# Cross-attention queries for pairs of tiles from float32r parts, rows normalised two tiles ahead, later weights loaded between the first contexts

## The chip, the core and the metric

The kernel runs on one core of a Trainium2 chip. The metric is the device time of one execution in microseconds (us). A core has TensorE (PE, with its weight loads shown as PEld), VectorE (DVE), ScalarE (ACT), GpSimd (POOL) and SyncE (SP), each with its own queue of instructions. They meet through semaphores only. SP and ACT issue the transfers from memory here.

## The reference

64 batches with 64 rows of x and 256 context rows each, 256 channels, 16 heads of 16. Three residual steps follow one another, all in float32:

```python
x = x + xattn(_layernorm(x), ctx, ctx, Wq, bq, Wk, bk, Wv, bv, Wo, bo)
x = x + attn(_layernorm(x), w_qkv, b_qkv, w_out, b_out)      # causal, 64 x 64
x = x + ffn(_layernorm(x), w_gate, w_up, w_down)             # quantised gate/up/down
# xattn
q = (queries @ Wq.T + bq).reshape(B, L, H, E)
k = (keys @ Wk.T + bk).reshape(B, S, H, E)
v = (values @ Wv.T + bv).reshape(B, S, H, E)
scores = jnp.einsum('blhe,bshe->bhls', q, k)
attn = jax.nn.softmax(scores * scale, axis=-1)
out = jnp.einsum('bhls,bshe->blhe', attn, v).reshape(B, L, H * E)
return out @ Wo.T + bo
```

## The kernel before

A tile is two batches, 128 rows; there are NT = 32 tiles. The kernel runs three stages after each other, each over all tiles: cross-attention, self-attention, feed-forward. x_all holds all rows between them. The order of the instructions on each engine is written out by hand, in one `body` per engine; no scheduler moves them. Every step waits for named semaphores.

In cross-attention a tile t has two halves s, one batch each. The steps of TensorE, by function, in the order of its `body(t)`:

- `pe_k` and `pe_v` (L287, L302) project a context half to keys and values. The context c_sb is split by `act_c` (L463, ScalarE) into a rounded float32r part ch, and by `pool_c` (L505, GpSimd) into the rest cl = c_sb - ch. Three products (high by high, high by low, low by high) then stand for the full one: 12 matmuls of 256 columns.
- `pe_xt` (L267) turns the normalised rows xn of tile t + 1. `act_xt` (L455) copies them to xnT, and `pe_q` (L274) makes q for the same tile with 8 fp32 matmuls of 128 columns. `dve_q` (L408) adds the bias, applies the head mask and writes qb in four operations.
- `pe_scores` (L318) writes four banks of scores, `dve_max` (L448) takes the maxima, `act_exp` (L488) makes eight exponentials with their sums, `pe_transpose` (L331) turns four pairs of them, `dve_pt` and `act_pt` (L417, L469) copy those to probsT.
- `pe_pv` (L354) multiplies by V; `pe_r` (L341) turns the inverse sums that `pool_rm` (L512) spreads; `dve_o` forms oT; `pe_out` (L364) projects it to y_ps and `dve_y` (L441) adds it to x_all.
- `dve_stats`, `pool_rstd` and `dve_xn` normalise x of tile t + 1 from the one buffer x_sb; `pool_xb` (L500) adds the output bias.

xt_ps and y_ps share one half of PSUM bank 3, q_ps is the other half. Beside this, tiles 1 to 6 sum the absolute feed-forward weights on ScalarE (`act_wabs`), tiles 9 to 20 round one piece of them each on VectorE (L558, L564, L569), and tiles 22 to 24 split the self-attention weights. SP issues x and the contexts for the next tile (L1076, L1082). Before its loop it issues the loads of the later stages, SET2 and SET3 (L1069, L1071), 4.3 MB.

## Time and profile before

| what | value |
|---|---|
| median of 3 runs | 943.34 us (943.32 to 947.49) |
| profiled execution, its own time | 944.46 us |
| its span, first to last instruction | 942.3 us |
| mean granted TensorE clock | 0.993 of 2.4 GHz |
| PE busy | 883.0 us, 94% |
| DVE busy | 774.7 us, 82% |
| ACT busy | 679.1 us, 72% |
| POOL busy | 408.9 us, 43% |
| transfers | 31.67 MB, mean 34 GB/s |

The share of busy time says which engine has the most work, not which one is waited for. The cross-attention stage fills the first 558 us of the span. The chain of work that the page follows back from the end covers 9% of the span, all in the last stage, so it says nothing of the stage that is changed; there the waits and the order in time have to be read.

### The profile page before, as it was taken

The page shows a single profiled execution, that of the slowest core. Times are in us where ns is not written, and L with a number is a line of the kernel's source. Part 1 is how long each engine was busy: PE and PEld are TensorE (multiplying, and loading weights), DVE is VectorE, ACT ScalarE, POOL GpSimd, SP SyncE. Part 2 cuts the span into 40 slices and gives each one's busy share as a digit, 9 for nine tenths or more (in the row PEclk, how much of TensorE's full clock was granted, in tenths as well). Part 3 has the DMA queues.
Part 4 walks back from the last instruction along what each step waited for, and adds up shares of the span by engine and source line. Part 5 has one row for each costly group of instructions (what it writes and reads, how often), then busy time and mean ns, then how long its engine had stood idle before and what let it go on. Part 6 is the DMA issues. An engine that isn't in the chain of part 4 may idle for free. (4 is left out here: it accounts for less than half of the span.)

```text
span 942.3 us, 28985 instructions
## 1 busy us (share of the span) xinstructions
PE 883.0 (94%) x9714; PEld 722.8 (77%) x9730; DVE 774.7 (82%) x1650; ACT 679.1 (72%) x2013; POOL 408.9 (43%) x611
## 2 busy tenths in 40 slices
PE   5899999999999999999999988999999995999996
PEld 4688888888888888888888876878878773555554
DVE  3787878888988888888888887988888886999995
ACT  3587787676776777767767675777777765888886
POOL 1222322223223222233332226766767642767775
PEclk9999999999999999999999999999999998999999
DMA  8111111111111111111111100000000000000010
GB/s 303 38 40 39 33 39 40 46 39 34 39 39 34 38 39 45 39 33 39 39 43 35 33 1 1 1 3 0 1 0 1 2 1 1 24 31 32 29 34 33
DMA packets 31623, 31.67 MB, mean 34 GB/s; under 512 B 3281, under 2 KB 30801, under 8 KB 31569
## 3 DMA queue, kind: packets, MB, share of 16 engines
q1 hardware_dynamic: 30720, 30.73, 10.6%
q8 instruction: 20, 0.33, 0.1%
q10 hardware_dynamic: 848, 0.33, 0.1%
q14 instruction: 35, 0.28, 0.1%
HBM read 26.86 MB, written 4.19 MB: 33 GB/s over the span
## 5 line engine op out<-in xcount | busy, mean ns | idle before, releaser
L488 ACT ACTIVATE probs<-psum,nmax 128x256 f32<-128x256 f32 x512 | 237.3, 488 | 90.1 <-DVE nmax L448 90.1
L448 DVE TENSOR_REDUCE nmax<-psum 128x2 f32<-128x512 f32 x256 | 159.0, 683 | 30.7 <-PE psum L318 30.7
L331 PE MATMUL psum<-id_sb,probs 128*128 128x128 f32 x1024 | 136.1, 276 | 14.1 <-ACT probs L488 14.0
L331 PEld LDWEIGHTS psum<-id_sb,probs 128*128 128x128 f32 x1024 | 111.6, 141 | 29.8 <-ACT probs L488 28.7
L496 POOL TENSOR_TENSOR rstd<-vare,minus_half 128x1 f32<-128x1 f32 x96 | 52.6, 548 | 183.9 <-DVE vare L385 181.3
L505 POOL TENSOR_TENSOR cl<-c_sb,ch 128x512 fp32r<-128x512 f32 x64 | 81.4, 1272 | 98.4 <-ACT ch L463 98.4
L488 ACT ACTIVATION_READ_ACCUMULATOR probs<-psum,nmax 128x1 f32 x512 | 112.7, 220 | 0.0
L469 ACT ACTIVATE probsT<-psum 128x512 f32<-128x512 f32 x160 | 90.7, 620 | 9.1 <-PE psum L331 9.1
L512 POOL TENSOR_TENSOR rm<-rinv,hm_sb 128x256 f32<-128x256 f32 x64 | 39.7, 620 | 129.0 <-DVE rinv L424 129.0
L318 PE MATMUL psum<-k_sb,qb 32*128 32x256 f32 x1024 | 78.4, 404 | 0.0
L354 PE MATMUL psum<-probsT,v_sb 128*32 128x128 f32 x2048 | 69.5, 277 | 0.0
L354 PEld LDWEIGHTS psum<-probsT,v_sb 128*32 128x32 f32 x2048 | 52.3, 110 | 21.4 <-issue 15.4
L395 DVE TENSOR_TENSOR v_sb<-psum,bv_sb 128x512 f32<-128x512 f32 x64 | 44.2, 691 | 24.1 <-PE psum L302 24.0
L417 DVE COPY probsT<-psum 128x512 f32<-128x512 f32 x96 | 62.7, 653 | 0.0
L1031 PE MATMUL psum<-wb_all,xqT 128*128 128x512 bf16 x240 | 58.9, 388 | 3.9 <-PEq L1058 2.6
L836 POOL TENSOR_TENSOR kbd<-c_sb,qm_sb 128x1024 f32<-128x1024 f32 x32 | 60.6, 1893 | 3.0 <-ACT c_sb L786 3.0
L318 PEld LDWEIGHTS psum<-k_sb,qb 32*128 32x128 f32 x1024 | 51.1, 186 | 11.2 <-issue 5.9
L302 PE MATMUL psum<-wvh,ch 128*128 128x256 f32 x256 | 59.5, 313 | 0.0
L455 ACT ACTIVATE xnT<-psum 128x256 f32<-128x256 f32 x32 | 12.2, 382 | 62.5 <-PE psum L267 62.5
L287 PE MATMUL psum<-ch,wkh 128*128 128x256 f32 x256 | 56.8, 303 | 0.0
L816 ACT ACTIVATE sc<-sc 128x1024 f32<-128x1024 f32 x32 | 33.8, 1058 | 28.0 <-DVE sc L741 28.0
L287 PE MATMUL psum<-cl,wkh 128*128 128x256 f32 x256 | 51.7, 284 | 0.0
(131 smaller groups left out, 2316.3 us busy)
## 6 DMA issues: line engine op xcount, KB each, us to landing
c_sb<-in_ctx_t SPq DMA_DIRECT2D x64, 256.0 KB, 2.7
x_sb<-in_x SPq DMA_DIRECT2D x32, 128.0 KB, 2.0
out<-y_sb SPq DMA_DIRECT2D x32, 128.0 KB, 1.7
w_all<-in_w_gate SPq DMA_DIRECT2D x1, 1024.0 KB, 8.6
w_all<-in_w_up SPq DMA_DIRECT2D x1, 1024.0 KB, 10.9
w_all<-in_w_down SPq DMA_DIRECT2D x1, 1024.0 KB, 13.1
wqkv_sb<-in_w_qkv SPq DMA_DIRECT2D x1, 768.0 KB, 6.5
wq_sb<-in_wq ACTq DMA_DIRECT2D x1, 256.0 KB, 3.8
```

Of the source, the lines that this page charges most:

```text
L287: last = nc.tensor.matmul(k_ps[:, m, :], w[:, k, cols], c[s][:, k, :], start=n + k == 0, stop=n == 2 and k == KT - 1)
L302: last = nc.tensor.matmul(v_ps[:, kh, :], c[s][:, k, keys], w[:, k, :], start=n + k == 0, stop=n == 2 and k == KT - 1)
L318: last = nc.tensor.matmul(sp[c][:, m * S:(m + 1) * S], qb[m][rows, s, :, :].rearrange("p h q -> p (h q)"), k_sb[rows, m, :], start=True, s ...
L331: last = nc.tensor.transpose(sp[g][:, c:c + P], probs[:, 2 * g + u, kh * P:(kh + 1) * P], id_sb[:])
L354: last = nc.tensor.matmul(op[32 * c:32 * c + 32, m * P:(m + 1) * P], v_sb[s][:, kh, 32 * j:32 * j + 32], probsT[:, 2 * c + m, kh, :], star ...
L417: nc.vector.tensor_copy(probsT[:, 2 * g:2 * g + 2, :, :].rearrange("p a b c -> p (a b c)"), sp[g]).then_inc(pt_dve, 1)
L448: nc.vector.tensor_reduce(nmax[:, 2 * g:2 * g + 2], sp[g].rearrange("p (u s) -> p u s", u=2), AX.X, ALU.max, negate=True).then_inc(max_don ...
L469: nc.scalar.activation(probsT[:, 2 * g:2 * g + 2, :, :].rearrange("p a b c -> p (a b c)"), sp[g], ACT.Copy).then_inc(pt_act, 1)
L488: nc.scalar.activation(probs[:, j, :], sp[g][:, u * S:(u + 1) * S], ACT.Exp, bias=nmax[:, j:j + 1], accum_out=rsum[:, j:j + 1]).then_inc(e ...
L505: nc.gpsimd.tensor_tensor(cl[s][:], c_sb[s][:], ch[s][:].bitcast(F32), ALU.subtract).then_inc(cl_done, 1)
L836: nc.gpsimd.tensor_tensor(kbd4[j][:], kT2[s][:, :, j * P:(j + 1) * P].unsqueeze(2).to_broadcast([P, KT, 4, P]), qm4_sb[:].unsqueeze(1).uns ...
L1031: last = nc.tensor.matmul(ps[n], xqT[:, k, :], w[:, k, n * 512:(n + 1) * 512], start=k == 0, stop=k == KT - 1)
```

## The change

**Queries for pairs.** Wq is split like Wk into wqh and wql. The turned rows are split too: `act_xt` copies them twice, to xnT and (rounded) to one half of x1h, and the new `pool_xl1` on GpSimd writes x1l = xnT - x1h. `pe_q` runs once for two tiles, in the odd ones, with 12 float32r matmuls of 256 columns over x1h and x1l; `dve_q` writes qb for both tiles in four operations of 256 columns. q_ps takes all of bank 3. xt_ps and y_ps move to the second half of bank 2, whose first half `pe_pv` writes; so `pe_pv` of half 0 now waits for the copy to x1h (x1h_done).

**Rows two tiles ahead.** x_sb becomes two buffers; statistics, normalising, turning and splitting run for tile t + 2. Loops take two tiles for each iteration. The last even tile (30) has none of it.

**Loads.** The identity and Wk come first on ScalarE's queue, x of tile 1 goes before Wv. SET2 follows the contexts of tile 1, and the three loads of SET3 follow those of tiles 2, 3 and 4, each with a semaphore of its own; the sums of absolute weights move to tiles 2 to 7. The first tile makes K, V and then q, instead of q first. kbd4 and sc of the second stage now lie in w_all and wait for the rounded weights (wq_step), which are ready in tile 20.

```diff
-        x_sb = sb("x_sb", [P, D])
+        x_sb = [sb(f"x_sb{j}", [P, D]) for j in range(2)]
+        x1h, x1l = sb("x1h", [P, KT, 2 * P], F32R), sb("x1l", [P, KT, 2 * P], F32R)
-        qb = [sb(f"qb{m}", [P, 2, 2, L]) for m in range(KT)]
+        qb = [sb(f"qb{m}", [P, 4, 2, L]) for m in range(KT)]
...
-        def pe_q(pe, t):
-            pe.wait_ge(xt_ev, t + 1)
+        def pe_q(pe, n):
+
+            pe.wait_ge(x1l_done, n * 2 + 2)
             for m in range(KT):
-                for k in range(KT):
-                    last = nc.tensor.matmul(q_ps[:, m, :], wq_sb[:, k, m * P:(m + 1) * P],
-                                            xnT[:, k, :], start=k == 0, stop=k == KT - 1)
+                cols = slice(m * P, (m + 1) * P)
+                for i, (w, x) in enumerate(((wqh, x1h), (wqh, x1l), (wql, x1h))):
+                    for k in range(KT):
+                        last = nc.tensor.matmul(q_ps[:, m, :], w[:, k, cols], x[:, k, :],
+                                                start=i + k == 0, stop=i == 2 and k == KT - 1)
             last.then_inc(q_mm, 1)
...
-        def pe_pv(pe, t, s):
+        def pe_pv(pe, t, s, ahead2=True):
+
             b = t * 2 + s
+            if s == 0 and ahead2:
+                pe.wait_ge(x1h_done, t + 3)
+            elif s == 0:
+                pe.wait_ge(y_ev, t)
...
-        def act_xt(a, t):
+        def act_xt(a, t, n, j, turned):
             a.wait_ge(xt_mm, t + 1)
-            nc.scalar.activation(xnT[:], xt_ps, ACT.Copy).then_inc(xt_ev, 1)
+            a.wait_ge(x1l_done, t)
+            nc.scalar.activation(xnT[:], turned, ACT.Copy).then_inc(xt_ev, 1)
+            a.wait_ge(q_mm, n)
+            nc.scalar.activation(x1h[:, :, j * P:(j + 1) * P], turned, ACT.Copy).then_inc(x1h_done, 1)
...
+        def pool_xl1(p, t, j):
+            p.wait_ge(xt_ev, t + 1)
+            p.wait_ge(x1h_done, t + 1)
+            cols = slice(j * P, (j + 1) * P)
+            nc.gpsimd.tensor_tensor(x1l[:, :, cols], xnT[:], x1h[:, :, cols].bitcast(F32),
+                                    ALU.subtract).then_inc(x1l_done, 1)
...
+                body(0, 0)
+                for dst, src in SET2:
+                    sp_.dma_start(dst, src).then_inc(w2_in, 16)
+                for i, (dst, src) in enumerate(SET3):
+                    body(1 + i, (1 + i) % 2)
+                    sp_.dma_start(dst, src).then_inc(w3_in[i], 16)
...
-                    pe_xt(pe, t + 1)
-                    pe_scores(pe, t, 1)
-                    pe_pv(pe, t, 0)
-                    pe_q(pe, t + 1)
+                    if ahead2:
+                        pe_xt(pe, t + 2, xt_ps)
+                    pe_scores(pe, t, 1, n, j)
+                    pe_pv(pe, t, 0, ahead2)
+                    if j == 1:
+                        pe_q(pe, n + 1)
                     pe_r(pe, t, 0)
                     pe_k(pe, t + 1, 0)
```

How the order changes on TensorE, between the scores of half 1 and K of the next tile. Before, in every tile (psum<-xnT,wq_sb is q, psum<-id_sb,rm the inverse sums):

```order
L318 MATMUL psum<-k_sb,qb 128x256 x4
L354 MATMUL psum<-probsT,v_sb 32x128 [waits pt_dve,pt_act,o_ev,v_ev]
L354 MATMUL psum<-probsT,v_sb 32x128 x15
L274 MATMUL psum<-xnT,wq_sb 128x128 [waits xt_ev]
L274 MATMUL psum<-xnT,wq_sb 128x128 x3
L341 MATMUL psum<-id_sb,rm 128x128 [waits v_ev,rm_done]
```

After, in an odd tile:

```order
L328 MATMUL psum<-k_sb,qb 128x256 x4
L369 MATMUL psum<-probsT,v_sb 32x128 [waits pt_dve,o_ev,pt_act,v_ev,x1h_done]
L369 MATMUL psum<-probsT,v_sb 32x128 x15
L284 MATMUL psum<-x1h,wqh 128x256 [waits x1l_done]
L284 MATMUL psum<-x1h,wqh 128x256
L284 MATMUL psum<-x1l,wqh 128x256 x2
L284 MATMUL psum<-x1h,wql 128x256 x2
L284 MATMUL psum<-x1h,wqh 128x256 x2
L284 MATMUL psum<-x1l,wqh 128x256 x2
L284 MATMUL psum<-x1h,wql 128x256 x2
L351 MATMUL psum<-id_sb,rm 128x128 [waits v_ev,rm_done]
```

In an even tile the L284 rows are missing: the inverse sums follow the product with V. (An fp32 matmul of the order is two in the trace.)

On GpSimd, one tile before, from the reciprocal root for the next rows to the rest of the second context half:

```order
L496 TENSOR_TENSOR rstd<-vare,minus_half 128x1 [waits xn_done,stats]
L512 TENSOR_TENSOR rm<-rinv,hm_sb 128x256 [waits r_mm,inv_done]
L500 TENSOR_TENSOR x_all<-x_sb,bo_sb 128x256 [waits x_in]
L505 TENSOR_TENSOR cl<-c_sb,ch 128x512 [waits ch_done]
L512 TENSOR_TENSOR rm<-rinv,hm_sb 128x256 [waits r_mm,inv_done]
L505 TENSOR_TENSOR cl<-c_sb,ch 128x512 [waits ch_done]
```

The same tile after:

```order
L512 TENSOR_TENSOR rstd<-vare,minus_half 128x1 [waits xn_done,stats]
L535 TENSOR_TENSOR rm<-rinv,hm_sb 128x256 [waits r_mm,inv_done]
L523 TENSOR_TENSOR x_all<-x_sb,bo_sb 128x256 [waits x_in0]
L518 TENSOR_TENSOR x1l<-xnT,x1h 128x2x128 [waits x1h_done,xt_ev]
L528 TENSOR_TENSOR cl<-c_sb,ch 128x512 [waits ch_done]
L535 TENSOR_TENSOR rm<-rinv,hm_sb 128x256 [waits r_mm,inv_done]
L528 TENSOR_TENSOR cl<-c_sb,ch 128x512 [waits ch_done]
```

x1l stands ahead of the first cl, for which K of the next tile waits.

TensorE at the start. Before, q and K of tile 0:

```order
L267 MATMUL psum<-id_sb,xn 128x128 [waits xn_done,wq_in]
L267 MATMUL psum<-id_sb,xn 128x128
L274 MATMUL psum<-xnT,wq_sb 128x128 [waits xt_ev]
L274 MATMUL psum<-xnT,wq_sb 128x128 x3
L287 MATMUL psum<-ch,wkh 128x256 [waits cl_done,ch_done,k_ev,wl_split,wh_split]
```

After, from the turned rows to V, behind which q(0) and the scores stand:

```order
L274 MATMUL psum<-id_sb,xn 128x128 [waits xn_done,id_in]
L274 MATMUL psum<-id_sb,xn 128x128
L297 MATMUL psum<-ch,wkh 128x256 [waits cl_done,k_ev,ch_done,wl_split]
...
L274 MATMUL psum<-id_sb,xn 128x128 [waits xn_done]
L274 MATMUL psum<-id_sb,xn 128x128
L312 MATMUL psum<-wvh,ch 128x256 [waits cl_done,v_ev,ch_done,wl_split]
```

K moved ahead of q and waits for its own weights only.

## Rows read from the trace of the kernel before

**Rows 1.** The waits: engine, line, releaser, us in total, times, longest.
```profile
PE psum L331 <- ACT probs L488: 14.0, 54, 0.3
```

**Rows 2.** Order in time, tile 29: start us, duration us, instruction, idle before.
```profile
515.04 1.15 PE L318 MATMUL psum<-k_sb,qb 32*128 32x256 f32 x16
...
520.71 0.25 ACT L488 ACTIVATION_READ_ACCUMULATOR probs<-psum,nmax 128x1 f32 x1
...
521.01 0.66 PE L331 MATMUL psum<-id_sb,probs 128*128 128x128 f32 x4 [0.26 <-ACT probs L488]
...
523.78 0.38 PE L267 MATMUL psum<-id_sb,xn 128*128 128x128 f32 x2
...
524.09 1.15 PE L318 MATMUL psum<-k_sb,qb 32*128 32x256 f32 x16
524.19 0.38 ACT L455 ACTIVATE xnT<-psum 128x256 f32<-128x256 f32 x1 [1.90 <-PE psum L267]
...
525.16 1.08 PE L354 MATMUL psum<-probsT,v_sb 128*32 128x128 f32 x32
525.17 1.28 POOL L505 TENSOR_TENSOR cl<-c_sb,ch 128x512 fp32r<-128x512 f32 x1 [1.89 <-ACT ch L463]
...
525.98 0.47 ACT L488 ACTIVATE probs<-psum,nmax 128x256 f32<-128x256 f32 x1 [0.88 <-DVE nmax L448]
526.17 1.16 PE L274 MATMUL psum<-xnT,wq_sb 128*128 128x128 f32 x8
...
527.17 0.38 PE L341 MATMUL psum<-id_sb,rm 128*128 128x128 f32 x2
...
527.31 0.48 PE L287 MATMUL psum<-ch,wkh 128*128 128x256 f32 x2
...
527.65 1.36 DVE L408 TENSOR_SCALAR qb<-psum,bq_sb,qm_sb 128x128 f32<-128x128 f32 x4
...
528.81 1.91 PE L331 MATMUL psum<-id_sb,probs 128*128 128x128 f32 x16
...
529.75 0.25 ACT L488 ACTIVATION_READ_ACCUMULATOR probs<-psum,nmax 128x1 f32 x1
...
530.47 0.48 PE L302 MATMUL psum<-wvh,ch 128*128 128x256 f32 x2
...
532.05 1.15 PE L318 MATMUL psum<-k_sb,qb 32*128 32x256 f32 x16
```

**Rows 3.** Groups by line over the span: busy us, mean ns of one, idle before.
```profile
L829 POOL TENSOR_TENSOR cl<-xnT,ch 128x256 fp32r<-128x256 f32 x32 | 24.0, 750 | 42.4 <-ACT ch L778 42.4
...
L778 ACT ACTIVATE ch<-psum 128x256 fp32r<-128x256 f32 x32 | 12.3, 383 | 0.0
...
L441 DVE TENSOR_TENSOR x_all<-psum,x_all 128x256 f32 (+1 forms) x32 | 13.6, 424 | 3.7 <-PE psum L364 2.9
```

**Rows 4.** Order in time, a tile with a weight piece.
```profile
309.59 0.68 DVE L400 TENSOR_TENSOR k_sb<-psum,bk_sb 128x512 f32<-128x512 f32 x1
...
310.50 1.06 PEld L318 LDWEIGHTS psum<-k_sb,qb 32*128 32x128 f32 x16
```

**Rows 5.** Order in time, the first 38 us.
```profile
5.50 1.26 POOL L505 TENSOR_TENSOR cl<-c_sb,ch 128x512 fp32r<-128x512 f32 x1 [0.63 <-ACT ch L463]
...
11.28 0.78 PE L287 MATMUL psum<-ch,wkh 128*128 128x256 f32 x2
...
15.25 1.15 PE L318 MATMUL psum<-k_sb,qb 32*128 32x256 f32 x16
...
21.00 0.66 PE L331 MATMUL psum<-id_sb,probs 128*128 128x128 f32 x4 [0.26 <-ACT probs L488]
...
24.62 0.43 DVE L378 BATCH_NORM_STATS2 stat<-x_sb 128x6 f32<-128x256 f32 x1 [5.73 <-DMA x_sb<-in_x]
...
27.77 2.09 PE L318 MATMUL psum<-k_sb,qb 32*128 32x256 f32 x16
...
37.01 1.15 PE L318 MATMUL psum<-k_sb,qb 32*128 32x256 f32 x16
```

More of the change, by code:

```diff
@@ L129, in block_kernel @@
         xh, xl = ch, cl
-        kbd4 = [sb(f"kbd4{s}", [P, KT, 4, P]) for s in range(2)]
         v2b = [sb(f"v2b{s}", [P, D]) for s in range(2)]
@@ L152, in block_kernel @@
         wd_b = wb_all[:, 8:12, :].rearrange("p a (c n) -> p (a c) n", c=2)
+        kbd4 = [w_all[:, 2 * i:2 * i + 2, :].rearrange("p k (h t) -> p k h t", h=4) for i in range(2)]
+        sc = w_all[:, 4:6, :].rearrange("p a (h l) -> p (a h) l", l=L)
         w_abs = sb("w_abs", [P, 12])
@@ L172, in block_kernel @@
         y_sb = [sb(f"y_sb{s}", [P, D]) for s in range(2)]
+        id_in = sem("id_in")
         wq_in = sem("wq_in")
-        wkv_in = sem("wkv_in")
+        wk_in = sem("wk_in")
+        wv_in = sem("wv_in")
         w1_in = sem("w1_in")
         w2_in = sem("w2_in")
-        w3_in = sem("w3_in")
+        w3_in = [sem(f"w3_in{i}") for i in range(3)]
         const_set = sem("const_set")
@@ L199, in block_kernel @@
                 (w_raw[2].rearrange("p (k n) -> p k n", k=IT), k_of(w_down))]
-        x_in = sem("x_in")
+        x_in = [sem(f"x_in{j}") for j in range(2)]
         c_in = [sem(f"c_in{s}") for s in range(2)]
@@ L318, in pe_scores @@
                     last = nc.tensor.matmul(sp[c][:, m * S:(m + 1) * S],
[L319 removed]
+                                            qb[m][rows, 2 * j + s, :, :].rearrange("p h q -> p (h q)"),
                                             k_sb[rows, m, :], start=True, stop=True)
@@ L1117, in body @@
                     pe_r(pe, t, 1)
-                body(0, True)
-                with pe.Fori(1, 8) as t:
-                    body(t, False)
-                body(8, False, wsum=True)
-                with pe.Fori(9, NT - 1) as t:
-                    body(t, False)
+                body(0, 0, 0, first=True)
+                pe.wait_ge(w1_in, 16 * len(SET1))
+                body(1, 0, 1)
+                with pe.Fori(1, 4) as n:
+                    body(n * 2, n, 0)
+                    body(n * 2 + 1, n, 1)
+                body(8, 4, 0, wsum=True)
+                body(9, 4, 1)
+                with pe.Fori(5, NT // 2 - 1) as n:
+                    body(n * 2, n, 0)
+                    body(n * 2 + 1, n, 1)
+                body(NT - 2, NT // 2 - 1, 0, ahead2=False)
                 t = NT - 1
@@ L1246, in body @@
                     dve_max(v, t + 1, 0)
-                body(0, True)
-                with v.Fori(1, 8) as t:
-                    body(t, False)
-                body(8, False, scale=True)
-                for i in range(12):
-                    body(9 + i, False, piece=i)
-                with v.Fori(21, NT - 1) as t:
-                    body(t, False)
+                body(0, 0, 0, first=True)
+                body(1, 0, 1)
+                with v.Fori(1, 4) as n:
+                    body(n * 2, n, 0)
+                    body(n * 2 + 1, n, 1)
+                body(8, 4, 0, scale=True)
+                for i in range(12):
+                    body(9 + i, (9 + i) // 2, (9 + i) % 2, piece=i)
+                body(21, 10, 1)
+                with v.Fori(11, NT // 2 - 1) as n:
+                    body(n * 2, n, 0)
+                    body(n * 2 + 1, n, 1)
+                body(NT - 2, NT // 2 - 1, 0, ahead2=False)
                 t = NT - 1
@@ L1349, in body @@
                     act_exp(a, t + 1, 0, (t, 1))
-                body(0)
+                body(0, 0, 0)
+                body(1, 0, 1)
                 for i in range(6):
-                    body(1 + i, (2 * i, 2 * i + 1))
-                with a.Fori(7, 22) as t:
-                    body(t)
-                for i in range(3):
-                    body(22 + i, w2=i)
-                with a.Fori(25, NT - 1) as t:
-                    body(t)
+                    body(2 + i, 1 + i // 2, i % 2, (2 * i, 2 * i + 1))
+                with a.Fori(4, 11) as n:
+                    body(n * 2, n, 0)
+                    body(n * 2 + 1, n, 1)
+                for i in range(4):
+                    body(22 + i, 11 + i // 2, i % 2, w2=i if i < 3 else None)
+                with a.Fori(13, NT // 2 - 1) as n:
+                    body(n * 2, n, 0)
+                    body(n * 2 + 1, n, 1)
+                body(NT - 2, NT // 2 - 1, 0, ahead2=False)
                 t = NT - 1
                 act_pt(a, t, 0)
-                a.wait_ge(q_mm, NT)
+                a.wait_ge(x1l_done, NT)
                 a.wait_ge(v_mm, 2 * NT - 1)
```

198 lines of the change are left out of this document (111 added, 87 removed).

## The prediction

> **What bounds the kernel now.** I name the work of tile t, batch half s by its scores matmuls (L318): S(t,s). I read the waits first, then one plain tile in order of time, then the start. The change touches the first stage only: the 32 tiles of cross-attention, 17.0 us each.
>
> TensorE (PE) is busy almost all the time, but it does not set the pace alone. The waits show it waiting for ScalarE's exponentials before the transposes of L331 [rows 1]. In tile 29 [rows 2] the order is S(29,0) at 515.04, S(29,1) at 524.09, S(30,0) at 532.05: 9.05 us and 7.96 us, 17.01 in all. Each window is a chain through four engines: scores, VectorE's maxima, eight exponentials on ScalarE, the transposes of the last probability pair, then V and the next scores. In the first window the last accumulator read starts at 520.71 and takes 0.25, so it ends at 520.96, and the last four transposes start at 521.01: S + 5.97. TensorE had been idle before them; the chain bounds this window.
>
> In the second window TensorE's own work fills the gap: scores 1.07, probabilities times V 1.01, q 1.00 (526.17 to 527.17), the r transposes 0.14, K 1.50 (527.31 to 528.81), then sixteen transposes in one run that lasts 1.66, from 528.81 to 530.47. The last four of them are the thirteenth to sixteenth, 12 x 0.104 = 1.25 after the first: 530.06, S + 5.97. ScalarE's last read ends at 529.75 + 0.25 = 530.00, S + 5.91, with some 0.05 for the signal: S + 5.96. So here **TensorE and ScalarE tie within about 0.05 us**. That tie is what the forecast rests on: taking q away from this window gives nothing, since the exponentials arrive when they did, and making q longer costs its full length.
>
> **The queries.** Before, every tile has eight 128x128 fp32 matmuls, 1.00 us in the row. After, every second tile (the odd ones) has twelve float32r matmuls of 256 columns and the even ones none. K's twelve matmuls have that shape and types: 1.50 us. Per pair TensorE falls from 2.00 to 1.50, 0.25 us a tile, and if TensorE were the bound, 15 pairs would give back 7.5 us. But the windows do not share: in an even tile the second window keeps its 7.96, by the exponentials, gain 0 (bounds 0 and the 0.05 of the tie). In an odd tile TensorE's run is 0.50 longer, and the tie takes about 0.03 off: 7.96 + 0.47. Fifteen pairs are computed in odd tiles 1, 3 ... 29: **15 x 0.47 = +7.0 us** (bounds 0.40 and 0.60, 6.0 and 9.0). Nothing later gives it back: the first window starts at the scores.
>
> The Trainium skill has another price for the removed matmuls. The rows say that eight fp32 matmuls of 128 columns take 1.00 us, 0.125 each, beside 0.125 for each of K's with 256 columns. FP8 and Floating Point Precision, TensorE Precision Notes, says that true FP32 makes four passes through the array; at the full clock an estimate by it is 8 x 4 x 128 / 2.4 GHz = 1.71 us a tile, and 12 x 256 / 2.4 GHz = 1.28 for the new pair. By that page odd windows would get shorter and the sum would lose its +7.0; the rows of both shapes disagree with it and decide.
>
> **What comes in beside it.** ScalarE copies the turned tile twice: the second copy is a row like L778, 383 ns [rows 3], about 0.28 after the first by the step from xnT at 524.19 to what follows it. The exponentials of this window start at 525.98 after 0.88 of idle time [rows 2], so it is hidden at 0; without that cover it would cost 0.28 in each even tile. It also gates probabilities times V (a new wait on x1h): the copy ends at about 524.19 + 0.28 + 0.38 = 524.85, against 525.16, hidden by 0.3. Behind that wait on TensorE stand pv, q, r and K.
>
> GpSimd gets the subtraction x1l, like L829, 750 ns [rows 3], ahead of cl of the next context, and K waits for cl. Before, cl starts at 525.17 and ends at 526.45. After, x1l runs from about 524.95 to 525.7, cl to 526.95 (1.28 long), K can start at about 527.1. In odd tiles K comes at 527.8 anyway: 0. In even tiles TensorE is ready at 526.3, waits to 527.1, runs K to 528.6 and reaches the last transposes at 529.85, against 530.06: still hidden, but by 0.2 only. A signal that takes 0.1 to 0.2 longer at each hop uses that up; I take +0.02 for each of 15, **+0.3 us** (bounds 0 and 0.15 each, 2.3).
>
> VectorE's four q operations per tile take 1.36 us; now four per pair of 256 columns. Another 256-column read of PSUM by VectorE takes 424 ns (L441) [rows 3], so four cost between 1.7 and twice 1.36, 2.7; I take 1.9, near the row. In most odd tiles VectorE has room. In tiles 9 to 20 it also carries a piece of the feed-forward weights: there K's copy starts at 309.59, ends at 310.27, and the scores start at 310.50 [rows 4], a margin of 0.23. After, q starts 0.25 later and lasts 0.5 longer, while TensorE moves by 0.47: it ends about 0.05 to 0.15 past. Six odd tiles of this kind: **+0.6 us** (bounds 0 and 3).
>
> The x load is issued a tile earlier into one of two buffers: its wait in SP's queue is for work long done: 0. The last even tile (30) loses its two x transposes, which stand in the first window behind the exponentials, 523.78 to 524.09 [rows 2]: **-0.3 us**.
>
> **The start.** Before, x of tile 1 stands in SP's queue behind the later weights (4.3 MB); VectorE waits for it until 24.62, and behind that on VectorE stand K's copy and the transposed probabilities, and S(0,1) comes at 27.77, 12.52 after S(0,0) at 15.25 [rows 5]. Its scores take 2.09 instead of 1.15, twice the time, as at 1.2 instead of 2.4 GHz, after TensorE's pause, and S(1,0) comes at 37.01, 9.24 later. After, x of tiles 1 and 2 are there in time. Tile 0 then goes: last transposes at 21.00, 5.75 after its scores; from them through V 1.99, as from 530.06 to 532.05, and 0.31 for x (523.78 to 524.09) [rows 2]: 8.05 from S(0,0) to S(0,1), and 7.96 to S(1,0). That is 16.0 instead of 21.76: -5.8. Against it the first scores: q(0) now stands behind V, and must be computed (1.5) and copied by VectorE (1.9) before them, 3.4 in all. K(0,0) can begin when cl is there, 6.76 in the row plus some 0.4 for one more load and a later copy, 7.1, where it began at 11.28: 4.2 earlier, but it and part of V run at the slow clock (K's first pair took 0.78 [rows 5], against 0.48 at 527.31 [rows 2]) and the x transposes of tile 1 stand between: 1.5 lost. 15.25 + 3.4 - 4.2 + 1.5 = 15.95, +0.7 (bounds 0 and +2.5). Start in all: **-5.1 us** (bounds -5.8 and -3.3). The later weights move between the contexts; the first of them is wanted in tile 2 and each has a tile's 17 us before its turn: 0.
>
> **Sum.** -5.1 + 7.0 + 0.3 + 0.6 - 0.3 = **+2.5 us**: span 942.3 to 944.8. The profiled run had 944.46, 2.2 around its span and 1.1 over the median of 943.34; the same on the median: **945.8**. Its own range, from 942.5 to 949.
>
> **Rivals.** (1) *TensorE is the bound and the tie is an illusion of modelled ends.* Then a pair saves 0.50: 15 x 0.5 = 7.5, 5.1 and 0.3: 943.3 - 12.9 = 930.4. For it: PE busy without a gap over the second window. Against: the 0.25 gaps before the transposes in the first window, and a chain of the same 5.97 in both. Chance 0.10. (2) *Slower: the subtraction on GpSimd makes cl late.* If cl ends more than 0.2 later than I place it (past 527.15 in the row's frame), K and then the last transposes slip in every even tile; at 0.3 to 0.5 each, 15 of them cost 4.5 to 7.5, less the 0.3 already taken: 950 to 953, take 951.5. For it: margin of 0.2 over three hops. Against: GpSimd idles 1.89 before cl. Chance 0.20. (3) *The start gives less than said*: the wait for q(0) leaves TensorE at 1.2 GHz, or the first scores come at 17.5 or later. Two to three us less: 948.3. Chance 0.12. The forecast has the rest, 0.58.
>
> **Numbers.** About 0.5% (4.7 us) is what a measurement of this kernel can tell from no change. Faster by more (under 938.6) is rival 1 and a little of the rest: 0.11. Slower by more (over 948.1): rival 2, half of rival 3, and the upper edge of the forecast: 0.29. Within: 0.60. The range for 8 in 10 is 941.0 to 952.0; it leaves out rival 1 and the far end of rival 2.
>
> **What the profile after would show.** Right: S to S in the second window 7.96 in even tiles and about 8.43 in odd ones; K in even tiles behind a wait of some 0.7 for cl, and the last four transposes still behind ScalarE; S(1,0) near 32. Wrong for the queries: second windows of 7.5 in even tiles (rival 1), or over 8.1 (rival 2). Wrong for the start: S(0,0) past 17, or a wait for x of tile 2.

## The result, and the profile after

The changed kernel takes **949.94 us** (median of 7 runs, 949.55 to 952.85) against 943.34 (7 runs, 941.7 to 947.49). The ratio is **1.0052, 95% interval 1.0033 to 1.0071**: slower by about half a per cent. The forecast was 945.8 with a range of 941 to 952, "within 0.5%" the likeliest case and slower given 0.29. The time lies inside the range, 4.1 above the forecast; the ratio is just over the bound of 0.5%, with an interval that reaches to both sides of it. The profiled execution has a span of 948.57 us, 6.23 more than before, at a mean granted clock of 0.990 (before: 0.993).

Where the 6.2 us come from, by the starts of the scores (now L328) and of the first instructions of the later stages in both traces:

| stretch | before | after | difference | forecast |
|---|---|---|---|---|
| to S(1,0) | 37.01 | 32.29 | -4.72 | -5.1 |
| second windows, 15 odd tiles | 7.96 to 8.29 | 8.49; 8.63 to 8.68 in tiles 11 to 19 | +8.12 | +7.0, +0.6 |
| second windows, 15 even tiles | 7.96 to 8.19 | 7.97 to 8.20 | +0.23 | +0.3 |
| first windows, tiles 1 to 31 | 9.04 to 9.11 | 9.05 to 9.12, tile 30 8.83 | +0.21 | -0.3 |
| S(31,1) to the first scores of self-attention | 14.29 | 15.71 | +1.42 | 0 |
| rest of self-attention | | | -0.47 | 0 |
| feed-forward, to its last tile | 138.60 | 139.31 | +0.71 | 0 |
| its end | 14.01 | 14.74 | +0.73 | 0 |

So in the stage that the change touches the balance is +3.8 (forecast +2.5), and behind it come +2.4 that the forecast had at 0. This is the difference of two single profiles. The rows of +1.42 and +0.73 are stretches in which TensorE was granted 1.2 instead of 2.4 GHz, and these are not shown to go with the kernel: over all its runs the changed kernel has a mean granted clock of 0.9904 (7 runs), the kernel before one of 0.9891 to 0.9895 in three later sets of runs (63 in all), whose medians are 944.88, 945.53 and 945.59. The profile of the kernel before, with 0.993, had more of the full clock than most of its runs. Against those medians the changed kernel is 4.4 to 5.1 us behind, about the 3.8 of the stage and 0.7 of the feed-forward steps (below); the two sides of this comparison were not measured together.

The waits of the kernel after (engine, line, releaser, us in total, times, longest). TensorE's wait for the exponentials is what it was in [rows 1], and the new wait for x1h is many small ones:

```profile
PE psum L341 <- ACT probs L504: 15.0, 56, 0.5
PEld psum L369 <- ACT x1h L471: 9.9, 30, 0.3
```

An odd tile in order of time (tile 29, both kernels' rows in [rows 2] and here: start, duration, instruction, idle before):

```profile
527.49 1.15 PE L328 MATMUL psum<-k_sb,qb 32*128 32x256 f32 x16
...
528.40 0.73 POOL L518 TENSOR_TENSOR x1l<-xnT,x1h 128x256 fp32r<-128x256 f32 x1 [2.03 <-ACT x1h L471]
528.57 0.81 PEld L369 LDWEIGHTS psum<-probsT,v_sb 128*32 128x32 f32 x32 [0.33 <-ACT x1h L471]
...
529.58 0.51 PE L284 MATMUL psum<-x1h,wqh 128*128 128x256 f32 x2
...
531.10 0.38 PE L351 MATMUL psum<-id_sb,rm 128*128 128x128 f32 x2
...
531.24 0.48 PE L297 MATMUL psum<-ch,wkh 128*128 128x256 f32 x2
...
532.74 1.91 PE L341 MATMUL psum<-id_sb,probs 128*128 128x128 f32 x16
533.16 0.25 ACT L504 ACTIVATION_READ_ACCUMULATOR probs<-psum,nmax 128x1 f32 x1
...
534.40 0.48 PE L312 MATMUL psum<-wvh,ch 128*128 128x256 f32 x2
534.54 0.68 DVE L414 TENSOR_TENSOR k_sb<-psum,bk_sb 128x512 f32<-128x512 f32 x1
```

The queries run from 529.58 to 531.10, 1.52 us, where they took 526.17 to 527.17, 1.00 us, in [rows 2]. K starts 3.75 behind the scores instead of 3.22, V 6.91 instead of 6.38: +0.53 at both. The last accumulator read of ScalarE starts 5.67 behind the scores, as before, so the exponentials are no later than they were. The window is longer by what the queries are longer, all of it. Probabilities times V wait for x1h in the weight loads, but start 1.08 behind the scores, as before (1.07).

An even tile (28), same columns:

```profile
510.46 1.15 PE L328 MATMUL psum<-k_sb,qb 32*128 32x256 f32 x16
...
512.13 1.27 POOL L528 TENSOR_TENSOR cl<-c_sb,ch 128x512 fp32r<-128x512 f32 x1
...
513.50 0.48 PE L297 MATMUL psum<-ch,wkh 128*128 128x256 f32 x2 [0.51 <-issue]
...
516.13 0.25 ACT L504 ACTIVATION_READ_ACCUMULATOR probs<-psum,nmax 128x1 f32 x1
...
516.85 0.49 PE L312 MATMUL psum<-wvh,ch 128*128 128x256 f32 x2
```

No queries are left there, and still V starts 6.39 behind the scores, as before. The last accumulator read starts 5.67 behind them (5.66 in [rows 2]). K waits until cl is done, 512.13 + 1.27 = 513.40, S + 2.94; the forecast had S + 2.86. The wait eats time that TensorE has over.

A tile with a weight piece (11):

```profile
220.78 0.42 DVE L587 TENSOR_SCALAR w_all<-w_all 128x512 f32<-128x512 f32 x1
...
222.45 0.51 DVE L592 TENSOR_SCALAR wb_all<-w_all 128x512 bf16<-128x512 f32 x1
...
222.88 0.68 DVE L414 TENSOR_TENSOR k_sb<-psum,bk_sb 128x512 f32<-128x512 f32 x1
...
223.79 0.53 PEld L328 LDWEIGHTS psum<-k_sb,qb 32*128 32x128 f32 x8 [0.27 <-issue]
```

K's copy ends at 223.56 and the scores start 0.23 later. In [rows 4] the same two stand 0.23 apart. In the plain tile 29 they were 0.76 apart (534.54 + 0.68 = 535.22, scores at 535.98). So the 0.23 that the prediction called a margin is the time from the copy's end to the scores, signal included, and no margin: VectorE was in a tie in those tiles already. The gap is 0.23 to 0.26 in tiles 8 to 20 of the kernel before, and 0.23 to 0.28 in odd tiles 11 to 19 of the changed kernel, although those windows are 0.7 us longer. (Tile 9 of the changed kernel shows 0.09, so the figure is not exact to the last tenth.)

The start, TensorE and VectorE:

```profile
7.55 0.79 PE L297 MATMUL psum<-ch,wkh 128*128 128x256 f32 x2 [1.44 <-DVE wkl L1249]
...
12.63 0.48 PE L284 MATMUL psum<-x1h,wqh 128*128 128x256 f32 x2
...
14.32 1.90 DVE L422 TENSOR_SCALAR qb<-psum,bq_sb,qm_sb 128x256 f32<-128x256 f32 x4 [0.91 <-PE psum L284]
16.28 1.15 PE L328 MATMUL psum<-k_sb,qb 32*128 32x256 f32 x16 [2.00 <-DVE qb L422]
...
24.26 1.15 PE L328 MATMUL psum<-k_sb,qb 32*128 32x256 f32 x16
...
32.29 1.15 PE L328 MATMUL psum<-k_sb,qb 32*128 32x256 f32 x16
```

The first scores come at 16.28 (forecast 15.95), behind the queries' 1.90 us on VectorE, as forecast. The 5.73 us wait for x of tile 1 in [rows 5] is gone, S(0,1) follows after 7.98 instead of 12.52, and its scores take 1.15 instead of 2.09.

Behind cross-attention, TensorE ahead of the first key projection of self-attention, kernel after and, below it, kernel before:

```profile
567.97 0.77 PE L666 MATMUL psum<-ch,w2h 128*128 128x256 f32 x2 [2.94 <-POOL cl L852]
568.54 0.63 PE L666 MATMUL psum<-cl,w2h 128*128 128x256 f32 x2
...
571.64 1.91 PE L341 MATMUL psum<-id_sb,probs 128*128 128x128 f32 x16
```

```profile
564.16 0.48 PE L643 MATMUL psum<-ch,w2h 128*128 128x256 f32 x2 [2.97 <-POOL cl L829]
564.48 0.40 PE L643 MATMUL psum<-cl,w2h 128*128 128x256 f32 x2
...
566.38 1.91 PE L331 MATMUL psum<-id_sb,probs 128*128 128x128 f32 x16
```

The pause is the same within 0.03 us, yet the nine pairs of matmuls behind it take 3.67 us after and 2.22 before. The stretches by time say why (stretch, its length, PE busy with the number of instructions, granted clock, share of the transfer engines, GB/s), kernel after and then before:

```profile
567.80:571.30 3.50, 3.33 (x16) 0.51 0.02 5
943.30:948.60 5.30, 1.65 (x8) 0.50 0.16 51
```

```profile
564.00:567.50 3.50, 3.34 (x29) 1.00 0.03 7
```

After the pause TensorE is granted 1.2 GHz for 3.4 us in the kernel after and 2.4 GHz in the kernel before. The end of the kernel after is in such a stretch too: its last down projection takes 1.78 us, where the same eight matmuls took 1.03 before. In the kernel before, such a stretch begins at 941.9, when its last matmul is done, so it costs nothing there.

### The profile page after: what moved, and what is told of

Its sections match the earlier page's. It is cut to its first block and busy times, and to the rows that moved or that the text cites. A ratio compares the mean times of both kernels' runs of the same rounds, so it can differ in the third digit from the quotient of the medians.

```text
span 948.6 us, 28405 instructions
## 1 busy us (share of the span) xinstructions
PE 883.4 (93%) x9650; PEld 717.2 (76%) x9666; DVE 761.9 (80%) x1587; ACT 691.1 (73%) x2046; POOL 431.6 (45%) x643
## 5 line engine op out<-in xcount | busy, mean ns | idle before, releaser
L341 PE MATMUL psum<-id_sb,probs 128*128 128x128 f32 x1024 | 139.0, 277 | 15.6 <-ACT probs L504 15.0
L328 PE MATMUL psum<-k_sb,qb 32*128 32x256 f32 x1024 | 77.3, 400 | 2.4 <-DVE qb L422 2.0
L859 POOL TENSOR_TENSOR w_all<-c_sb,qm_sb 128x1024 f32<-128x1024 f32 x32 | 60.6, 1894 | 4.2 <-ACT c_sb L809 4.2
L328 PEld LDWEIGHTS psum<-k_sb,qb 32*128 32x128 f32 x1024 | 50.5, 184 | 13.6 <-issue 6.6
L445 DVE TENSOR_TENSOR o_prod<-psum,r_sb 128x256 f32<-128x256 f32 x64 | 27.1, 423 | 41.2 <-issue 35.1
L839 ACT ACTIVATE w_all<-w_all 128x1024 f32<-128x1024 f32 x32 | 33.8, 1058 | 27.4 <-DVE w_all L764 27.4
```

The lines of the kernel that those rows point to most:

```text
L328: last = nc.tensor.matmul(sp[c][:, m * S:(m + 1) * S], qb[m][rows, 2 * j + s, :, :].rearrange("p h q -> p (h q)"), k_sb[rows, m, :], start ...
L341: last = nc.tensor.transpose(sp[g][:, c:c + P], probs[:, 2 * g + u, kh * P:(kh + 1) * P], id_sb[:])
L859: nc.gpsimd.tensor_tensor(kbd4[j][:], kT2[s][:, :, j * P:(j + 1) * P].unsqueeze(2).to_broadcast([P, KT, 4, P]), qm4_sb[:].unsqueeze(1).uns ...
```

## The experiments

Three theories stood. **A**: the forecast's own, a tie of TensorE and ScalarE in the second window, so that longer queries cost their length and no queries give nothing; the start gives back 5. **B** (rival 1): TensorE is the bound. **C** (rival 2): the subtraction x1l makes cl late. Behind them a fourth question came with the trace: whether the loss behind cross-attention is the clock of TensorE.

**The early weights alone.** The kernel before, with the later weights issued between the first contexts and the sums of the absolute weights one tile later; the queries untouched.

```diff
-                for dst, src in SET2:
-                    sp_.dma_start(dst, src).then_inc(w2_in, 16)
-                for dst, src in SET3:
-                    sp_.dma_start(dst, src).then_inc(w3_in, 16)
-                with sp_.Fori(0, NT - 1) as t:
...
+                body(0)
+                for dst, src in SET2:
+                    sp_.dma_start(dst, src).then_inc(w2_in, 16)
+                for i, (dst, src) in enumerate(SET3):
+                    body(1 + i)
+                    sp_.dma_start(dst, src).then_inc(w3_in[i], 16)
+                with sp_.Fori(4, NT - 1) as t:
```

> The kernel before with one part of the change: the later weights (SET2, SET3) are issued between the first contexts, and the sums of absolute weights move to tiles 2 to 7. Queries stay per tile, x one tile ahead, the first tile in its old order. Theory (the start of the changed kernel gained by this alone): no wait for x of tile 1, scores of tile 0 half 1 about 8.0 us after those of half 0 instead of 12.5, the next at 7.96 instead of 9.24, so 5.8 us less in all: 937.5. Rival (the gain came from x two tiles ahead and K ahead of q, since x of tile 1 must wait for the output bias, which lands at 11.4): 0 to 2 us less: 942.

Measured: 940.07 us, ratio 0.9946 (0.9930 to 0.9962). S(0,0) at 15.28, S(0,1) 7.96 later, S(1,0) at 31.26, the windows 9.05 and 7.96. The start gives 5.75 us of trace, where 5.8 was expected. The profiled span fell by 3.4 only: this profile has a stretch at 1.2 GHz in the key projection (from 559.65) and is 1.6 us longer there than the profile of the kernel before, which has none. The median fell by 4.8 (before was 944.88 on that chip), to 2.6 above the 937.5 expected. The start's part is **shown**, and this part of the change is faster by itself.

**The queries shorter and longer.** Half of the product left out; and one contraction done twice.

```diff
-                for k in range(KT):
-                    last = nc.tensor.matmul(q_ps[:, m, :], wq_sb[:, k, m * P:(m + 1) * P],
-                                            xnT[:, k, :], start=k == 0, stop=k == KT - 1)
+                last = nc.tensor.matmul(q_ps[:, m, :], wq_sb[:, 0, m * P:(m + 1) * P],
+                                        xnT[:, 0, :], start=True, stop=True)
```

> The kernel before with half of the query product left out (one of the two contractions of 128 channels), so TensorE has 0.50 us less in every tile. Theory (exponentials and TensorE tie in the second window): the window stays at 7.96 or falls by at most 0.05: 941.5 to 943.5. Rival (TensorE is the bound of the stage): 31 windows shorter by 0.50: 927.8.

```diff
-                for k in range(KT):
+                for i, k in enumerate((0, 1, 1)):
```

> The kernel before with one contraction of the query product done twice, so TensorE has 0.50 us more in every tile. Theory (the tie leaves no slack): 31 windows longer by 0.47 to 0.53, 14.6 to 16.4 more: 958 to 960. Rival (TensorE has slack in the second window and the changed kernel's longer odd windows come from somewhere else, the copy or the subtraction): within 2 us of 943.3.

Measured: 945.26 us with half of it, ratio 1.0006 (0.9993 to 1.0019), second windows 7.96 to 7.98 in plain tiles. With half more, 958.3 us, ratio 1.0139 (1.0120 to 1.0159), second windows 8.41 (8.63 in tile 8). TensorE in the second window of tile 28 with the short queries, then of tile 29 with the long ones:

```profile
508.47 0.71 PE L273 MATMUL psum<-xnT,wq_sb 128*128 128x128 f32 x4
509.02 0.38 PE L340 MATMUL psum<-id_sb,rm 128*128 128x128 f32 x2
...
510.66 1.47 PE L330 MATMUL psum<-id_sb,probs 128*128 128x128 f32 x12
512.36 0.66 PE L330 MATMUL psum<-id_sb,probs 128*128 128x128 f32 x4 [0.23 <-ACT probs L487]
```

```profile
538.40 1.60 PE L274 MATMUL psum<-xnT,wq_sb 128*128 128x128 f32 x12
539.85 0.38 PE L341 MATMUL psum<-id_sb,rm 128*128 128x128 f32 x2
```

With half of the queries gone, the last four transposes wait 0.23 for ScalarE and start 5.98 behind the scores (506.38), where the forecast put them at S + 5.97 with all the queries there. That is the tie, and **B is dead**: it had 927.8 for this run. The starts also price the queries: 0.55, 1.00 and 1.45 us for 4, 8 and 12 records of 128 columns, so 0.45 for four more, and the window grew by those 0.45. No slack was left in the tie. The other side of it is as plain: half of the queries' work gone from every window gave nothing.

**The pair with two products.** The changed kernel without its third product (low part of Wq). Eight records instead of twelve; in the trace they take 1.05 us, near the 1.00 of before.

```diff
-                for i, (w, x) in enumerate(((wqh, x1h), (wqh, x1l), (wql, x1h))):
+                for i, (w, x) in enumerate(((wqh, x1h), (wqh, x1l))):
...
-                                                start=i + k == 0, stop=i == 2 and k == KT - 1)
+                                                start=i + k == 0, stop=i == 1 and k == KT - 1)
```

> The changed kernel with the third product of the query left out (low weights by high rows), 8 float32r matmuls for a pair instead of 12, 1.00 us as before the change. Theory (the odd windows are long by the length of q alone): odd windows 7.97 to 8.0 instead of 8.49, weight-piece ones back too, 15 x 0.5 to 0.6: 941 to 942. Rival (GpSimd's subtraction or VectorE's wider q copies set the odd window): odd windows stay over 8.3: 947 or more.

Measured: 944.28 us, ratio 0.9989 (0.9975 to 1.0002). That is above the 941 to 942 expected. Odd windows 8.03 in plain tiles, 8.22 in tile 9, 8.38 in tiles 11 to 19. In plain odd tiles the whole loss but 0.07 is the length of the twelve matmuls; here the expectation, 7.97 to 8.0, nearly held. The piece tiles were expected to come back too, and did not: 0.35 more is left, although TensorE has nothing more to do there than in the others. VectorE sets the time in those.

**The weight pieces later.** The changed kernel, with a piece's clip and cast moved behind the last maxima of the tile.

```diff
-                    if piece is not None:
-                        dve_wclip(v, piece)
...
-                    if piece is not None:
-                        dve_wcast(v, piece)
...
+                    if piece is not None:
+                        dve_wclip(v, piece)
+                        dve_wcast(v, piece)
```

> The changed kernel with the second and third step of each weight piece on VectorE moved behind the last maxima of the tile, out of the window that has the q copies. Theory (VectorE's copies make odd windows of tiles 11 to 19 8.63 instead of 8.49): those five windows at 8.49, 0.7 us less: 949.2. Rival (the extra 0.14 comes from TensorE or from the shared memory): windows stay at 8.63.

Measured: 949.9 us, ratio 1.0047 (1.0030 to 1.0063), not below the changed kernel. But the windows did what was expected: odd ones in tiles 11 to 19 take 8.49 instead of 8.63, the same as in plain tiles. The rows of tile 11 there:

```profile
222.61 0.68 DVE L414 TENSOR_TENSOR k_sb<-psum,bk_sb 128x512 f32<-128x512 f32 x1
224.14 0.31 PEld L328 LDWEIGHTS psum<-k_sb,qb 32*128 32x128 f32 x8
```

0.85 between copy and scores instead of 0.23. The 0.8 us that this gives are outweighed in the profiled run by more stretches at 1.2 GHz in the last stage (from 787.6, 794.4 and 808.1, where up to its end the changed kernel has one, from 796.5), so the total decides nothing here; the windows do.

**The subtraction twice.** The changed kernel with the subtraction on GpSimd done once more, into a free tile.

```diff
+            nc.gpsimd.tensor_tensor(qT2[j][:, :, cols], xnT[:], x1h[:, :, cols].bitcast(F32),
+                                    ALU.subtract)
```

> The changed kernel with the subtraction on GpSimd done twice (the first into an unused buffer), 0.7 us more ahead of cl. Theory (in even tiles K waits for cl with only 0.1 to 0.2 us of margin to the exponentials): even second windows 7.97 become 8.5 to 8.6, 15 x 0.55 = 8 more: 958; odd ones stay at 8.49 to 8.6. Rival (GpSimd has room, cl is far from the path): even windows stay, 950.

Measured: 960.35 us, ratio 1.0152 (1.0130 to 1.0175). Even windows 8.46, odd ones 8.78 in plain tiles. GpSimd and TensorE in tile 28, whose scores start at 521.65:

```profile
524.01 1.26 POOL L530 TENSOR_TENSOR cl<-c_sb,ch 128x512 fp32r<-128x512 f32 x1
...
525.38 0.48 PE L297 MATMUL psum<-ch,wkh 128*128 128x256 f32 x2 [1.20 <-issue]
...
528.53 0.48 PE L312 MATMUL psum<-wvh,ch 128*128 128x256 f32 x2
```

K starts 3.73 behind the scores instead of 3.04, 0.69 later, and the even window is 0.49 longer: 0.20 of the delay was free. **Rival C's mechanism is real**, and its threshold is 0.2 past the present end of cl (S + 3.14; the forecast put it at S + 3.06); the changed kernel stays on the near side. Odd windows grow too, by 0.29 where at most 0.1 was expected: there the queries wait for x1l (0.22 in tile 29), and the time is 2.4 over the 958 expected.

**Filling the pause.** Identity transposes into a free part of PSUM, 24 of them, in TensorE's pause ahead of the first key projection of self-attention. First on the kernel with the early weights alone, then on the changed kernel and on the kernel before.

```diff
+                for i in range(24):
+                    nc.tensor.transpose(mp[:, 0:P], id_sb[:], id_sb[:])
```

> e1_start_only with 24 transposes of the identity into a free PSUM bank, about 2.6 us of TensorE work in the pause of 2.9 us before the first key projection of self-attention. In e1, in the changed kernel and in two other experiments that projection falls into a stretch at half clock (granted clock 0.5 for 3.4 us), in the kernel before it does not. Theory (the pause brings the slow stretch, and it costs about 1.4 us there): no half-clock stretch near 560 us, 1 to 1.5 us less than e1: 938.8. Rival (the stretch comes anyway or its cost is hidden by the subtraction on GpSimd): the same as e1 within 0.3 us.

> The changed kernel with 24 transposes of the identity into a free PSUM bank, put on TensorE in its pause of 2.94 us ahead of the first key projection of the self-attention (567.97 us in the changed kernel's trace, where 3.41 us at half clock follow). Theory, that the changed kernel's loss behind the cross-attention is the clock after that pause: the stretch at half clock is gone, the first scores of the self-attention come 3.84 us behind the last cross scores as before and not 5.26, and the time is 1.4 to 3 us below the changed kernel's 949.9, so 947 to 948.5; the odd tiles' 8.5 us and the start stay as they are, so that it is still 2.5 to 5 us behind the kernel before. Rival, that the later rows hang on something else (arrival of the key weights, the subtraction ahead of the projection): the first scores stay 5.26 us behind and the time at 949.9.

> The kernel before with the same 24 transposes in its pause of 2.97 us ahead of the first key projection (564.16 us in its trace, with no slow stretch right behind it, one at 580.07 us). Theory: since the projection runs at full clock there already, the gain is only that of the later stretch, 0 to 2 us, so 941.3 to 943.5. Rival, that the filling gains 2.9 us in this kernel as it did in the one with the early weights: 940.5; then the changed kernel's extra 1.4 us would not be a difference in clock but chance of one profile.

Measured:

| kernel | without | with the filling | ratio to before, with it |
|---|---|---|---|
| early weights alone | 940.07 | 937.17 | 0.9907 (0.9888 to 0.9926) |
| the changed kernel | 949.94 | 946.50 | 1.0025 (1.0011 to 1.0039) |
| the kernel before | 945.59 | 943.36 | 0.9983 (0.9969 to 0.9998) |

(The first two rows set medians of different occasions side by side; the kernel before had 944.88 and 945.53 beside the two numbers of the first row, 943.34 and 945.59 beside those of the second. The ratios, each to the kernel before on its own chip, are the firmer numbers.) Not all that was expected holds. With the early weights the gain is 2.9, where 1 to 1.5 was expected; in that profile two slow stretches are gone, not one. The changed kernel with the filling was expected at 947 to 948.5 and came below, and it is 0.9 behind the kernel before without the filling, not 2.5 to 5. (The 3.84 and 5.26 named there are the lags of the changed kernel behind the kernel before at S(31,1) and at the first scores of self-attention, not times from one to the other.) For the kernel before, the gain of 2.2 lies between the theory, 0 to 2, and the rival, 2.9. TensorE in the changed kernel with the filling, and the clock behind it:

```profile
564.57 2.78 PE L1182 MATMUL psum<-id_sb 128*128 128x128 f32 x24
567.47 0.50 PE L666 MATMUL psum<-ch,w2h 128*128 128x256 f32 x2
567.81 0.40 PE L666 MATMUL psum<-cl,w2h 128*128 128x256 f32 x2
```

```profile
567.40:570.90 3.50, 3.43 (x29) 1.00 0.00 0
584.00:588.00 4.00, 3.89 (x38) 1.00 0.00 0
```

Both stretches at 1.2 GHz are gone in this profile, the one behind the pause and the one 17 us later. From S(31,1) to the first scores of self-attention it is now 14.08 us instead of 15.71; with the early weights alone it was 15.89, and 14.10 with the filling. In the kernel before the same filling leaves that stretch of the trace nearly as it was (14.08 against 14.29), and its profiled span is 940.6 mainly because the first scores come at 14.34 instead of 15.25. Its median moved by 2.2 us, ratio 0.9983. With the filling in both, the changed kernel is 3.1 us behind (946.50 against 943.36), near the +3.8 of its stage.

So the +1.4 us between the two profiles **is the clock** behind the pause: shown. That it is a cost of the change is **not shown**, and the profiles speak against it. The same pause, 2.93 to 2.97 us, is in all nine profiles without the filling. The slow stretch stands right behind it in six of them, among these both variants of the kernel before with other query lengths (from 563.9 and 577.1), and not in three: the kernel before, the keys first, and the changed kernel with the subtraction twice. The stretch some 17 us later (15 to 19 behind the first key matmul) is in all nine, the kernel before too (580.1). With the filling the first stretch is gone in all five profiles, the second in two only. The mean granted clock of all runs agrees that the filling works in each kernel: it rises from 0.9908 to 0.9940 with the early weights, from 0.9904 to 0.9928 in the changed kernel, from 0.9891 to 0.9912 in the kernel before. In the ratios the gain stands clear of the intervals for the early weights; for the changed kernel they overlap. What decides in a single run whether the slow stretch comes, these runs do not show.

**Keys first, and two fillings more.** Early weights, and at the start the keys ahead of the queries on TensorE and on VectorE, with the identity and Wk loaded first:

```diff
+                pe.wait_ge(id_in, 16)
+                pe_xt(pe, 0)
+                pe.wait_ge(wl_split, 1)
+                pe_k(pe, 0, 0)
                 pe.wait_ge(wq_in, 16 * len(SET_Q))
...
+                a.dma_start(id_sb[:], ident).then_inc(id_in, 16)
+                a.dma_start(wk_sb[:], k_of(wk)).then_inc(wk_in, 16)
```

> e1_start_only with the changed kernel's start on top: identity and Wk first on ScalarE's queue, each weight with its own semaphore, K of the first half ahead of q, but q still the fp32 one of tile 0 alone, behind K and ahead of V. Theory (what delayed the changed kernel's first scores to 16.28 was q(0) for two tiles and its copy, not the loads): first scores at 13.0 to 13.5 instead of 15.28, 2 us less than e1: 938. Rival (loads or the slow clock at the start bound it): first scores at 15 or later, the same as e1.

> The kernel before with the later weights loaded between the first contexts, the keys ahead of the query at the start, and the 24 transposes in the pause ahead of the first key projection. Theory, that the two gains add (the start 0.5 to 1.5 us below the version with early weights alone, the filling 2.9 us): 936.0 to 937.5. Rival, that the stretches at half clock only move to another place when one is filled: 938 to 940.

And with 22 and 12 transposes more around the seam to the last stage:

```diff
+                for i in range(22):
+                    nc.tensor.transpose(bank[1][:, 0:P], id_sb[:], id_sb[:])
...
+                for i in range(12):
+                    nc.tensor.transpose(bank[1][:, 0:P], id_sb[:], id_sb[:])
```

> As the last, and 22 more transposes ahead of the first query of the last stage's cross part and 12 behind the last output projection, in the pauses at 778 to 785 us behind which the gate and up projections run at half clock for 6.8 us. Theory, that these 6.8 us at half clock cost half of what TensorE does in them where nothing else limits: 1 to 1.5 us less than without them, 934.5 to 936.5. Rival, that TensorE has slack there or the transposes come too early or too late to hold the clock: no gain, 936 to 937.5; if they push work back, up to 1 us slower.

Measured: 940.17 (ratio 0.9934, 0.9916 to 0.9953), 936.47 (0.9904, 0.9877 to 0.9931) and 938.48 (0.9930, 0.9910 to 0.9949). Keys first brings S(0,0) to 13.94 (13.0 to 13.5 was expected), and no gain in the median over the early weights alone (940.07). With the filling it is 936.47, beside 937.17 without the keys first: the intervals overlap, so the keys are not shown to help. The last two fillings **lost** 2.0 us, more than either expectation allowed: every run with them is slower than every run without, though the intervals of the two ratios overlap. The profiled spans differ by 1.2 (935.2 against 934.0). The rest lies outside the span: the time is 2.3 to 4.1 us above the span in the runs with these fillings and 2.1 to 2.2 without, for which the runs show no cause. TensorE there without them, then with them:

```profile
785.34 3.19 PE L1033 MATMUL psum<-wb_all,xqT 128*128 128x512 bf16 x7 [2.65 <-PEq L1060]
...
793.07 1.09 PE L1044 MATMUL psum<-id_sb,hq 128*128 128x128 f32 x8 [1.54 <-POOL hq L983]
```

```profile
785.43 1.67 PE L1033 MATMUL psum<-wb_all,xqT 128*128 128x512 bf16 x7 [1.17 <-PEq L1060]
...
792.91 1.62 PE L1044 MATMUL psum<-id_sb,hq 128*128 128x128 f32 x8 [2.05 <-POOL hq L983]
794.32 0.64 PE L1020 MATMUL psum<-id_sb,xq 128*128 128x128 f32 x2
794.75 1.92 PE L1053 MATMUL psum<-wb_all,hqT 128*128 128x256 bf16 x8
```

The gate products ran at full clock, 1.67 instead of 3.19 us, and the next step came 0.16 us earlier, since it waits for GpSimd. The half-speed stretch then began at 793.3, on the down projection (1.92 us for what takes 1.03 at full clock), where TensorE has no slack: the first four tiles took 22.20 us instead of 21.23. Full clock came where it was free anyway, half clock where it counts.

The best of these, 936.5 to 937.2 us with the early weights and the one filling, beats both kernels, the one before by 0.9 to 1.0% and the changed one by about 1.4%.

## Why the prediction was right or wrong

- **The tie** (right in kind, 0.06 a window too generous). Even windows 7.97 to 8.03, forecast 7.96: right. Odd windows 8.49 in plain tiles, forecast 8.43. The step that took 0.03 of tie off a length of 0.50 failed in both factors: the queries take 1.52 against 1.00, so 0.52, and nothing of it is hidden. The fp32 run with a third contraction shows the same, window and queries both +0.45. The 15 odd windows sum to +8.12, where +7.0 and +0.6 were forecast.
- **The count of the fp32 matmuls** (wrong, without effect). The prediction, and the description of the kernel ahead of it, said "eight fp32 matmuls of 128 columns". The loops of L274 issue four; each is two records in the trace, as the description of the change says of the order. The rows of before show 1.00 us for the whole and that carried the sum. But the sentence on the Trainium skill was wrong by the factor of two. By the Trainium skill, FP8 and Floating Point Precision, TensorE Precision Notes, true FP32 makes four passes: four matmuls of 128 columns are an estimate of 4 x 4 x 128 / 2.4 GHz = 0.85 us, and the pair's twelve of 256 columns one of 1.28. The measured increment, 0.45 for two more fp32 matmuls, agrees with the 0.43 of this estimate; the twelve took 1.52. By the page too the odd windows get longer, and the prediction was wrong to say that the rows disagree with it.
- **VectorE in the piece tiles** (right in kind; the margin misread). The forecast took 0.23 between copy and scores for slack. It is the delay from copy to scores, found in both kernels in just these tiles; so VectorE was already in the tie, and its longer query copy costs about 0.15 more in each of five tiles, 0.8 us in all, where 0.6 was forecast for six. Moving the piece away removes it.
- **GpSimd in even tiles** (right). cl ends at S + 2.94, forecast S + 2.86; the room left is 0.20, forecast 0.2. Rival 2 did not occur, and with one subtraction more it does.
- **The x1h wait, ScalarE's second copy, the x loads** (right, 0). V and probabilities times V start where they did.
- **The start** (right; 4.72 for 5.1). The first scores were 0.3 later than placed. The removal of the wait is worth 5.75 alone; that the queries come behind V costs about 1.0.
- **Tile 30** (-0.22 for -0.3). The other 30 first windows are up to 0.07 longer, +0.43 together, which the forecast did not have.
- **Later stages at 0** (+2.4 between the two profiles; wrong by 0.7 for the kernel, the rest is not the kernel's as far as is known). The clock behind the pause ahead of the key projection costs 1.4 in this profile, and goes away with the filling; the last down projection at 1.2 GHz costs 0.7. Both come and go between profiles of either kernel, and over all runs the changed kernel has no lower clock than the kernel before. The third part, +0.71, is three steps of 0.24 in the feed-forward stage, 8 tiles apart. They stand in the same three tiles of all five profiles of the changed program and its variants, in which the last 27 steps take 118.14 to 118.20 us. None of the nine profiles of the kernel before and its variants has these three (117.42 to 117.46); two, those with the early weights alone, have one of 0.28, in the first of these tiles (117.70). So they go with the program, not with the run. VectorE's reciprocal (L952) starts 0.25 late there, with nothing that it waits for being late; the cause is **open**, and no run was made for it.

The forecast named no rival for the clock behind pauses, though both mean clock and the slices of the page were at hand. Its 945.8 was 4.1 too low. By the two profiles that is 1.3 from the windows and the start, 2.4 from behind them, and the rest from how the profiled run stands to the median. By all runs it is the 1.3, the 0.7 of the steps, and some 2 because the forecast built on 943.34, which is 1.5 to 2.3 below the medians of the kernel before in its later sets. That the term for VectorE came out near, 0.8 for 0.6, is in part luck, since it was worked out from a margin that was not there.

## What to carry to other kernels

Where two engines tie in a window, a saving on one of them gives nothing, even if it is made in every window (half of the queries gone: ratio 1.0006). Work gathered in every second window is worse than that: the saving is lost in half of them and the added length is paid in full in the others. A gap between a producer's end and its consumer's start is no margin until a tile with plenty of time shows a larger one. Work that TensorE does for nothing in a pause can be worth more than the work that was optimised, where the stretch behind the pause is on the path; the one try elsewhere put the slow stretch onto one that is. A difference of clock between two profiles is the change's only if the clocks of all the runs differ too.

## What the runs showed of the hardware

- A pause of 2.93 to 2.97 us on TensorE was followed by 3.4 us at 1.2 GHz in six of nine profiles (from its first matmul, or up to 1.5 us behind it) and by full clock in three. 2.78 us of transposes in the pause kept full clock behind it in five of five; a second stretch some 17 us later, in all nine, was gone in two of the five. The Trainium skill, TensorE: Matmul & The Clock Gate, Part 1: The HAM clock gate, gives the same two levels, 1.2 GHz when idle and 2.4 when busy. All records of these traces are at one or the other.
- In the key projection the slow clock made TensorE's 18 matmuls 1.45 us longer and the next stage's first scores 1.4 later; at the gate products, behind which TensorE waits for GpSimd, it made them 1.52 us longer and the next step 0.16 later.
- An fp32 matmul of 128 columns added 0.225 us, both its records together (0.45 for two more), and a float32r matmul of 256 columns 0.12 (1.52 for twelve, 1.05 for eight).
